# A transformer block for 16 batches on one core: the order of loads and weight preparation ahead of batch 0

## The reference, cut to what matters

```python
x = x + 0.5 * ffn(layernorm(x))
x = x + attention(layernorm(x))      # 16 heads of 16, rope on q and k, softmax, output projection
x = x + 0.5 * ffn(layernorm(x))
# ffn(x), for each batch:
base = x @ W_base + b_base
h = relu(x @ W_enc[n] + b_enc[n])                    # 8 autoencoders n
recon = h @ W_dec[n] + b_dec[n]
n = argmin over n of mean((recon - x) ** 2)          # the adapter for this batch
out = base + relu(x @ W_down[n] + b_down[n]) @ W_up[n] + b_up[n]
```

## Time and profile before

| what | value |
|---|---|
| median of 3 timed runs | 2045.04 us (2039.3 to 2045.09) |
| the profiled execution | 2036.09 us |
| its span, first to last instruction | 2034.3 us |
| PE busy | 1819.5 us, 89% |
| DVE busy | 1287.8 us, 63% |
| ACT busy | 986.9 us, 49% |
| POOL busy | 516.8 us, 25% |
| mean granted TensorE clock | 0.967 |
| DMA packets, bytes | 96685, 99.72 MB |

### The profile page before, as it was taken

How to read it: one execution, slowest core, us unless ns; L and a number is a source line. 1 busy time by engine, 2 the same in 40 slices (tenths; PEclk the granted TensorE clock), 3 DMA queues, 4 the chain that set the end, 5 groups by cost and what they waited for, 6 DMA issues and landing times.

```text
span 2034.3 us, 29855 instructions
## 1 busy us (share of the span) xinstructions
PE 1819.5 (89%) x9128; PEld 999.1 (49%) x9128; DVE 1287.8 (63%) x2796; ACT 986.9 (49%) x1953; POOL 516.8 (25%) x664
## 2 busy tenths in 40 slices
PE   2669898999989999899989999899998999998885
PEld 1543545555454545445455554545455454544344
DVE  6357665766757676666757667576766766665631
ACT  0125465555635555454545556355553645464541
POOL 3131314141221414122141412214141221413101
PEclk9879999999999999899999999999998999999897
DMA  4050505032150503205050321405041050504100
GB/s 105 11 94 11 94 11 96 9 66 50 29 88 12 104 4 74 41 19 97 12 105 1 66 50 31 86 12 104 12 72 35 23 93 12 104 1 89 16 11 11
DMA packets 96685, 99.72 MB, mean 49 GB/s; under 512 B 19970, under 2 KB 88195, under 8 KB 96387
## 3 DMA queue, kind: packets, MB, share of 16 engines
q1 hardware_dynamic: 96516, 97.66, 25.5%
HBM read 63.54 MB, written 33.55 MB: 48 GB/s over the span
## 4 chain that ended last, share of the span: by engine, by line
PE 62%; DVE 11%; DMA 9%; issue 8%; ACT 4%; SPq 4%; POOL 2%; POOLq 0%; DVEq 0%; ACTq 0%
PE ps L510 10%; PE ps L498 9%; PE ps L577 8%; PE ps L488 8%; PE ps L556 6%; DMA scratch<-parts 5%; DVE mx L816 5%; PE ps L565 4%; PE ps L613 4%; SPq L473 3%; DMA out_dram<-x 3%; PE ps L629 3%; PE ps L674 2%; ACT pr L709 2%; PE ps L616 2%
## 5 line engine op out<-in xcount | busy, mean ns | idle before, releaser
L816 DVE TENSOR_REDUCE mx<-ps 128x1 f32<-128x512 f32 x1024 | 655.0, 685 | 271.4 <-PE ps L488 268.8
L709 ACT ACTIVATE pr<-ps 128x512 f32<-128x512 f32 x1024 | 555.9, 598 | 284.8 <-PE ps L498 284.2
L488 PE MATMUL ps<-stack 96*128 96x512 bf16 x1024 | 326.8, 388 | 58.6 <-issue 34.0
L498 PE MATMUL ps<-stack 98*128 98x512 bf16 x1024 | 320.7, 384 | 19.5 <-ACT pr L709 10.4
L510 PE MATMUL ps<-pr,va 128*32 128x512 f32 x2048 | 272.5, 604 | 4.6 <-ACT pr L709 4.6
L762 ACT ACTIVATE h<-ps,benc 128x512 f32<-128x512 f32 x128 | 88.0, 687 | 271.6 <-PE ps L556 271.6
L498 PEld LDWEIGHTS ps<-stack 98*128 98x128 bf16 x1024 | 77.6, 100 | 269.3 <-ACT pr L709 173.0
L488 PEld LDWEIGHTS ps<-stack 96*128 96x128 bf16 x1024 | 96.8, 98 | 218.7 <-DVE mx L816 89.3
L868 DVE SCALAR_TENSOR_TENSOR ps<-ps,wb,h 128x512 f32<-128x512 f32 x128 | 96.7, 756 | 149.9 <-PE ps L565 149.9
L1009 POOL TENSOR_SCALAR rs<-mv 128x4 f32<-128x4 f32 x48 | 11.5, 241 | 651.0 <-DVE mv L836 651.0
L556 PE MATMUL ps<-xh,w_eh 128*128 128x512 f32 x256 | 121.1, 473 | 17.8 <-issue 11.3
(11 more groups left out here) (155 smaller groups left out, 2995.1 us busy)
## 6 DMA issues: line engine op xcount, KB each, us to landing
stack<-scratch SPq DMA_DIRECT2D x384, 128.0 KB, 4.4
scratch<-parts SPq DMA_DIRECT2D x64, 384.0 KB, 5.4
xin<-in_L_attn_x_dram SPq DMA_DIRECT2D x16, 512.0 KB, 3.5
out_dram<-x SPq DMA_DIRECT2D x16, 512.0 KB, 6.0
stack<-wu_mT SPq DMA_DIRECT2D x128, 4.0 KB, 1.7
cst<-in_const_dram SPq DMA_DIRECT2D x1, 1024.0 KB
raw<-in_L_ffn_W_dec_dram SPq DMA_DIRECT2D x1, 512.0 KB, 5.5
pr<-in_L_ffn_W_enc_dram SPq DMA_DIRECT2D x2, 256.0 KB, 5.5
```

Source lines behind the costliest of these rows:

```text
L488: pe.matmul(bank1[:, t % 2, :], stack[b.odd][0][0:KB, hd, 128 * t:128 * t + 128], stack[b.odd][1][0:KB, hd, :], start=True, stop=True).the ...
L498: pe.matmul(bank2[:, a % 2, :], stack[b.odd][1][:, 4 * g + a, 128 * t:128 * t + 128], stack[b.odd][0][:, 4 * g + a, :], start=True, stop=T ...
L709: act.activation(pr[:, n % 2, a, :], bank2[:, a % 2, :], ACT.Exp, scale=SCALE).then_inc(ex_done.sem, 1)
L816: dve.tensor_reduce(mx[:, hd // 4 % 2, e:e + 1], bank1[:, t % 2, :], AX.X, ALU.max).then_inc(mx_done.sem, 1)
```

## The change

- The loads of the first group get semaphores of their own. SP issues x, the tables (s_ident), both parts of W_enc and benc (s_enc), then the 18 loads of s_rest. ScalarE issues W_dec, both parts of bdec and cidx (s_decoder).
- The two rows of -1 in stack are no longer filled by GpSimd. GpSimd fills 2 x 256 elements, and two transfers at the end of SP's opening copy them out (s_rows). TensorE and ScalarE wait for these ahead of the first L498 and the first maxima.
- ScalarE makes w_eh, as soon as W_enc is there; VectorE makes w_el.
- The rest of VectorE's opening becomes two steps of the walk of pass -1: w1 (decoder weights, cidx, b_base) ahead of the first decoder product, and w2 (splits of W_base, Wq, Wk, Wv) behind the choice. The waits for s_split move to the first up product (2) and the first q product (3).
- GpSimd's remaining fills stand ahead of its work on rs.

```diff
@@ schedule
+            if at == (2, 0) and initial(n): step("w1")       # behind zs, ahead of gr
             if at == (6, 1):
                 step("cost", n, 0)
                 step("pick", n, 0)
+                if initial(n): step("w2")
@@ macaron
+        minus = mT[0:2].rearrange("p k q -> p (k q)")
@@ sync
-                bring(s_first, cst[:, 0:tables], const[:, 0:tables])
-                bring(s_first, benc[:], b_enc.rearrange("(p e) r -> (e r) p", e=2))
-                bring(s_first, cidx[:].bitcast(I32), connected_idx.partition_broadcast(128))
...
+                bring(s_ident, cst[:, 0:tables], const[:, 0:tables])
+                for c in range(C):
+                    bring(s_enc, w_e[:, c], W_enc[:, 128 * c:128 * c + 128, :].rearrange("n p r -> p n r"))
+                bring(s_enc, benc[:], b_enc.rearrange("(p e) r -> (e r) p", e=2))
...
+                sp.wait_ge(s_fill, 1)
+                for o in range(2):
+                    bring(s_rows, stack[o][1][KB:KB + 2, :, :].rearrange("p h (a x) -> p (h a) x", x=2 * 128),
+                          minus.unsqueeze(1).to_broadcast([2, 2 * H, 2 * 128]))
@@ tensor
+                if initial(b) and n == 0 and half == 0:      # s2
+                    pe.wait_ge(s_rows, 32)
...
-            pe.wait_ge(s_first, 16 * FIRST_LOADS)
+            pe.wait_ge(s_ident, 16)
+            pe.wait_ge(s_decoder, 16 * DECODER_LOADS)
@@ scalar
+            act.dma_start(w_dec, W_dec.rearrange("(a b) r d -> (b r) a d", b=2)).then_inc(s_decoder, 16)
+            with nc.allow_non_contiguous_dma(reason="small bias columns, once"):
+                for c in range(C):
+                    act.dma_start(bdec[:, c], b_dec[:, 128 * c:128 * c + 128].rearrange("n p -> p n")).then_inc(s_decoder, 16)
+                act.dma_start(cidx[:].bitcast(I32), connected_idx.partition_broadcast(128)).then_inc(s_decoder, 16)
+            act.wait_ge(s_enc, 16 * ENC_LOADS)
+            act.copy(w_eh[:], w_e).then_inc(s_high, 1)
             enter(do)
@@ vector
+            def decoder_weights():          # w1
+                # ident_b, w_dh, w_dl, bd_sum, gram_w filled with 0, wait s_wt 2, wb2 and gram_w (16 small
+                # copies), power, s_ready 1, cidx, wait s_rest, wu_all + b_base, s_ready 2
+            def dense_weights():            # w2
+                # w_bh, w_bl, s_split 2, then the pairs of Wq, Wk, Wv, s_split 3
             dve.memset(power[:], -0.5).then_inc(s_const, 1)
-            dve.wait_ge(s_first, 16 * FIRST_LOADS)
-            link(dve.tensor_copy(ident_b[:], ident))
             enter(do)
...
+            dve.wait_ge(s_decoder, 16 * DECODER_LOADS)
             link(dve.tensor_scalar(bdec[:], bdec[:], -2.0, None, ALU.mult))
             dve.wait_ge(s_wt, 1)
             link(dve.tensor_copy(raw[:, 2, :], ps[:, 0, :]))
             dve.tensor_copy(raw[:, 3, :], ps[:, 1, :]).then_inc(s_dec, 1)
...
+            dve.wait_ge(s_high, 1)
+            dve.tensor_tensor(w_el[:], w_e, w_eh[:].bitcast(F32), ALU.subtract).then_inc(s_split, 1)
             walk(dve, do)
@@ gpsimd
+            pool.memset(minus, -1.0).then_inc(s_fill, 1)
+            pool.wait_ge(s_fill, 1)
+            pool.memset(mid[R:R + 1, :], 1.0).then_inc(s_fill, 1)
+            pool.wait_ge(s_fill, 2)
+            pool.memset(va[:, :, :, HD:2 * HD], 1.0).then_inc(s_fill, 1)
             pool.wait_ge(s_const, 1)
             enter(do)
-
-            pool.wait_ge(*rs_done[0].at(Batch(0, 0), 0))
-            pool.memset(mid[R:R + 1, :], 1.0).then_inc(s_fill, 1)
...
-                pool.memset(stack[o][1][KB:KB + 2, :, :], -1.0).then_inc(s_fill, 1)
```

More of the change, by code:

```diff
@@ L401, in macaron @@
         passed = sem("passed")
-        s_first = sem("s_first")
+        s_ident = sem("s_ident")
+        s_enc = sem("s_enc")
+        s_decoder = sem("s_decoder")
         s_rest = sem("s_rest")
+        s_rows = sem("s_rows")
+        s_high = sem("s_high")
         s_const = sem("s_const")
@@ L411, in macaron @@
         s_ready = sem("s_ready")
-        FIRST_LOADS, REST_LOADS = 8, 18
+        ENC_LOADS, DECODER_LOADS, REST_LOADS = 3, 4, 18
+        w_dec = raw[:, 0:2, :].rearrange("p a (b c) -> p (a b) c", c=D)
+        w_decT = raw[:, 2:4, :]
         block = ctx.enter_context(nc.Block())
@@ L622, in project @@
                 if k == 0:
+                    if initial(b):
+                        pe.wait_ge(s_split, 3)
                     pe.wait_ge(*xl_done[2].at(b, C - 1))
@@ L721, in maxima @@
                 bank = late
+                if initial(b) and g == 0:
+                    act.wait_ge(s_rows, 32)
                 act.wait_ge(*mt_full.at(b, g))
@@ L950, in out_project @@
                    .then_inc(x2_done.sem, 1)
+            def decoder_weights():
+                link(dve.tensor_copy(ident_b[:], ident))
+                link(dve.tensor_scalar(w_dh[:], w_decT, -2.0, None, ALU.mult))
+                link(dve.scalar_tensor_tensor(out=w_dl[:], in0=w_decT, scalar=-2.0, in1=w_dh[:].bitcast(F32), op0=ALU.mult,
+                                              op1=ALU.subtract))
+                sq = key[0]
+                link(dve.tensor_tensor(sq[:], bdec[:], bdec[:], ALU.mult))
+                link(dve.tensor_tensor(bd_sum[:], sq[:, 0, :], sq[:, 1, :], ALU.add))
+                link(dve.tensor_scalar(bd_sum[:], bd_sum[:], S / 4.0, None, ALU.mult))
+                link(dve.memset(gram_w[:], 0.0))
+                dve.wait_ge(s_wt, 2)
+                for p in range(NP):
+                    for e in range(2):
+                        q = slice(R * e, R * e + R)
+                        dve.tensor_scalar(wb2[q, p:p + 1], ps[q, 3, 10 * p + e:10 * p + e + 1], -1.0, None, ALU.mult)
+                        dve.tensor_copy(gram_w[q, p, R * e:R * e + R], ps[q, 2, 128 * p + R * e:128 * p + R * e + R])
+                link(dve.tensor_copy(power[:], power[:]))
+                dve.tensor_copy(power[:], power[:]).then_inc(s_ready, 1)
+                link(dve.tensor_copy(z[0][:], cidx[:].bitcast(I32)))
+                link(dve.tensor_scalar(z[1][:], z[0][:], 0.0, float(N), ALU.is_lt, ALU.mult))
+                link(dve.tensor_tensor(z[0][:], z[0][:], z[1][:], ALU.add))
+                link(dve.tensor_scalar(cidx[:], z[0][:], 0.0, float(N - 1), ALU.max, ALU.min))
+                dve.wait_ge(s_rest, 16 * REST_LOADS)
+                dve.tensor_tensor(wu_all[R:R + 1], wu_all[R:R + 1],
+                                  x2[R:R + 1, 0:1, :].to_broadcast([1, N, D]), ALU.add).then_inc(s_ready, 1)
@@ new lines, in dense_weights @@
+            def dense_weights():
+                link(dve.tensor_copy(w_bh[:], w_b))
+                dve.tensor_tensor(w_bl[:], w_b, w_bh[:].bitcast(F32), ALU.subtract).then_inc(s_split, 1)
+                for raw_w, w in ((q_raw, w_q), (k_raw, w_k), (v_raw, w_v)):
+                    link(dve.tensor_copy(w[0][:], raw_w))
+                    last = dve.tensor_tensor(w[1][:], raw_w, w[0][:].bitcast(F32), ALU.subtract)
+                    if w is not w_v:
+                        link(last)
+                last.then_inc(s_split, 1)
@@ L962, in _ @@
-            dve.tensor_tensor(w_el[:], w_e, w_eh[:].bitcast(F32), ALU.subtract).then_inc(s_split, 1)
+            dve.wait_ge(s_decoder, 16 * DECODER_LOADS)
             link(dve.tensor_scalar(bdec[:], bdec[:], -2.0, None, ALU.mult))
[L965 to L968, removed]
             dve.wait_ge(s_wt, 1)
```

21 lines of the change are left out of this document (5 added, 16 removed).

## The result

| | before | after |
|---|---|---|
| median of the timed runs | 2042.17 us (4: 2036.6 to 2045.09) | 2004.75 us (4: 2002.29 to 2008.66) |
| ratio of the times | | 0.9818, 95% interval 0.9801 to 0.9836 |
| the profiled execution, its span | 2036.09, 2034.3 us | 2006.59, 2004.8 us |
| first encoder matmul of batch 0 | 54.12 us | 18.51 us |
| first down matmul (L599, now L608) | 77.99 us | 40.87 us |

The kernel is 37.4 us faster; 33.9 were forecast, and a time of 2010.

The account below looks back on a forecast made before the run. The prediction took the opening's chain of waits up to batch 0's first encoder matmul as what the change could shorten: 34.0 - 0.6 + 0.5 = 33.9 us saved, 2045.0 less that 2011.1, said as 2010, range 2000 to 2022.

Parts of the forecast that it names:

- The sum: Whole kernel: 34.0 us from the opening, less 0.6, plus 0.5, makes 33.9 us saved; time given as 2010.
- Part 1, the fill: Four xn normalisations in the opening: without GpSimd's fills beside them 1.6 us instead of 15.76, so 14.2 us go.
- Rival C: Opening's xn stall is not the fill's but DMA traffic's: 21 us saved, time 2024; chance 0.03.
- Part 2, the loads: Opening's loads: x at 4.6, decoder group at 9.0, first encoder matmul at 20.1 instead of 54.12, 34.0 us saved.
- rival A: Opening's loads come no earlier, since two queues share the engines: 29.5 to 31 us saved, 2014 to 2016; chance 0.13.
- The cover of xl and w_el: Ahead of the first encoder matmul: xl ready at about 16.6 and w_el at 13.3, both 3 us early.
- Parts 2 and 5, TensorE's rate: Gram products 7.0 us as now; first encoder matmuls start less slowly without the pause, gain 0 to 2.0, taken 0.5.
- Part 3, w1: Decoder weights inside VectorE's walk: hidden, 5.9 us of cover on TensorE, 4 us ahead of VectorE's first decoder product.
- rival B: Hidden work comes out, by late rest loads or the choice beside the splits: 3 to 6 us less saved; chance 0.08.
- Part 4, w2: Dense weight splits behind the choice: hidden, but slow GpSimd's choice instructions by 0 to 2.3 us, taken 0.6.
- Rival D, the seams: Seams between batches run longer at 1.2 GHz: slower, 6 us more each at half rate gives 2056; chance 0.04.

Follow-up runs that it names:

- second traces: The kernel before and the kernel after, each run again unchanged: 2042.38 us (ratio 1.0001) and 2005.35 us (ratio 0.9826).
- one queue: Kernel after, but SyncE issues all loads, W_dec, bdec and cidx behind the tables and ahead of W_enc: 1999.97 us, run again 2004.99 us.
- fills alone: Kernel before, with GpSimd's two fills of 2 x 8192 replaced by two transfers and its other fills ahead of rs: 2030.22 us, ratio 0.9945.
- pause: Kernel after, with one VectorE copy ahead of the Gram products made four times, for 2.1 us more: 2005.81 us.
- halves: Kernel after, x split over both queues, first transposes awaiting W_dec and tables, benc on ScalarE's queue, Wq, Wk, Wv splits behind the choice: 2007.42 us, ratio 0.9839.
- weight work ahead: Kernel after, with both weight steps (w1 and w2) called ahead of VectorE's walk, ahead of xl: 2022.16 us, run again 2019.58 us.

## Why the prediction was right, point by point

**The sum.** 33.9 us forecast, 37.4 measured (interval 33.5 to 40.6 by the ratio), and the sign, the place and the mechanism were as said. The first down matmul came 37.1 us earlier, and in the second traces 78.52 - 41.29 = 37.2. The 37.1 are 35.6 to the first encoder matmul (54.12 - 18.51; 34.0 forecast), 2.1 in the encoder (0.5 forecast) and 0.6 given back at the choice. The 35.6 are two errors of opposite sign on the forecast start of 20.1: the transposes began 2.0 us late and took 0.5 less, and the Gram products took 3.1 less. So part of the nearness is luck. The medians with the traces' openings taken off show no loss behind the opening (an estimate, since only the profiled executions have a known opening): 2042.5 - 1.8 - 78.3 = 1962.4 us of body before, 2005.35 - 1.8 - 41.1 = 1962.5 after. The 2010 was 5.3 too high: 3.5 from the gain, 2.9 from a median of before that came out as 2042.2 instead of 2045.0, less the 1.1 by which 2010 was set under the sum.

**Part 1, the fill.** Right: xn 1.39 us, and both ways of testing it gave 13.6 to 14.3 us in the trace for 14.2. Rival C (the stall is the load traffic's) is out. The Trainium skill's page SBUF — State Buffer, section "SBUF: two separate sides", has VectorE and GpSimd share one pair of ports there, one holding it while the other waits; of VectorE's instructions with one input it says this for those that run in a two-port mode. These traces agree on the wait, with 15.76 us beside the fills and 1.38 without; the mode of an instruction stands in none of them.

**Part 2, the loads.** The term that was mis-sized in one direction: x was taken at 4.6 and came at about 6.0, the decoder group at 9.0 and came at 10.9. On this landing rival A (12.0) was nearer than the forecast (9.0), though not on the time. x took 5.3 us to land where it had taken 3.5. The 4.6 rested on ScalarE needing 1.46 us to issue W_dec; it needed 0.51, and x came at the forecast's own upper bound, 6.1, at which W_dec's 512 KB travel beside it. The bytes fit: the DMA engines moved 1130 KB up to the landing of x, which is about x, W_dec and the tables, and 700 KB with one queue, where x took 3.7 us (view by stretch, the kernel after, then one queue):

```profile
1.50:6.04 4.54, 0.00 (x0) 0.00 (x0) 0.00 (x0) 0.00 (x0) 1.07 (x2) 1.00 0.83 249
```

```profile
1.50:4.40 2.90, 0.00 (x0) 0.00 (x0) 0.00 (x0) 0.52 (x1) 1.08 (x2) 1.00 0.77 241
```

What the small loads add to that isn't separated. With all loads on one queue x was earlier, and so were the first transposes, which wait for the decoder group (9.39 and 10.10 against 11.05 and 11.19). So the second queue brought nothing to these two (W_enc it brought 0.9 us sooner); what the opening won from the loads is left to their order and to what each engine waits for. The cover of xl and w_el, taken as 3 us, was 1.0 (xl done at 17.49, the Gram products at 18.5).

**Parts 2 and 5, TensorE's rate.** The term that was mis-sized in the other direction, and it outweighed the first. The Gram products were taken at 7.0 us "as now", with 0.5 us for the encoder. They took 3.9, and the encoder 5.86 instead of 7.96 (the chain shows 5.71, since it gives the first 0.15 us to the Gram products). That is 2.1 us, a little more than the 2.0 that the forecast allowed at most, and 5.2 us together for the 0.5. The earlier trace rows had shown that TensorE worked slowly at first after a pause, and "the Gram products themselves never sped up" was read as a property of theirs, without asking what the 2.0 us pause ahead of them did. Over all traces: with a pause of 2 us or more directly ahead, the Gram products took 7.0 us in 5 of 5 (before twice, fills alone, pause, halves); with transposes running into them they took 3.7 to 4.5 in 7 of 9 and about 7.0 in 2 of 9, and both of these kernels had quick ones in their other trace. So a pause is enough for slow Gram products as far as five traces can show it, and it is not the only thing that gives them. The moment of the rise to the 2.4 GHz level (0.69 for four matmuls against 1.20) differs from execution to execution of one kernel. What decides it isn't shown.

**Part 3, w1.** Right in kind, thin in size. The forecast had 5.9 us of cover ahead of the first decoder matmul and 4 ahead of VectorE's first decoder product. With the faster TensorE, and VectorE's part done at about the forecast time, the first shrank to 25.2 - 23.8 = 1.4 us and the second to 27.85 - 27.39 = 0.5. In the one-queue kernel the second was gone, which is rival B: of the 1.8 us by which its first encoder matmul was earlier, 1.1 were lost by the first down matmul.

**Part 4, w2.** Right: 0.6 us taken, 3.06 - 2.46 = 0.60 measured, and moving the splits gave it back. That it fits to the tenth is luck, since the bounds were 0 and 2.3.

**Rival D, the seams.** It did not turn the sign, but the body varies more than was thought. The bodies of all traces lie between 1955.7 and 1967.6 us, and those of one kernel 0.0 to 4.7 apart. This is why the two spans of the table differ by 29.5 us and the medians by 37.4: the first trace of before has a body of 1956.3, the first of after 1963.9. In the second pair of traces the spans differ by 34.3; both profiled executions of before were under the median of their kernel (2036.09 and 2041.27), both of after above it (2006.59 and 2006.98). An example of low clock is one stretch near the end of the kernel after:

```profile
1840.00:1880.00 40.00, 29.05 (x91) 12.50 (x91) 22.43 (x43) 11.80 (x27) 5.65 (x11) 0.66 0.38 63
```

The mean granted clock was 0.966 and 0.967 in the traces with bodies of 1955.9, 1956.3 and 1958.5 us and 0.962 to 0.964 in those with 1963.9, 1964.4 and 1967.6, but also 0.961 in one with 1959.4 (weight work ahead, second trace) and 0.965 in the shortest, 1955.7 (one queue, first trace). So long bodies mostly go with a lower clock, but what fixes either for an execution stays open, and so does why the kernel with the pause lost 6.9 us in its opening and only 1.1 in its time.

**Where the 37.1 us came from**, by the traces: 14 from the fills and 16 from the weight work inside the walk (part of it TensorE's slow start, which comes back with the pause), each measured by putting it back into the kernel after. The remaining 7 or so fall to the loads' order, the earlier wait for x and the faster Gram products; this is a remainder, since no run puts the old load order back, and the three are not told apart.

## What to carry to other kernels

In an opening, order the work by what the next engine waits for and look for the wait, not for the busy share: of the 37 us here 14 were VectorE held by a neighbour's fill, and some 16 VectorE work that nobody wanted yet. When a gap in front of TensorE closes, cost the work behind the gap anew, since a duration measured after a pause may be of the lower clock. Covers shrink with it: take the slack from the faster schedule, not from the old one.

## What the runs showed of the hardware that was not expected

- GpSimd's fill of two partitions x 8192 elements took 6.96 us, and that of 128 partitions x 1024 elements 0.98 us: here (bf16 in the one, f32 in the other) the time went by the elements along the partition and not by their sum. The long one held a VectorE instruction of 0.40 us for its whole length (7.1 us).
- The holding goes the other way too. In the eight traces in which VectorE's b_base add of 2.28 us (L998) overlapped GpSimd's offsets, one of these took 2.2 to 2.35 us beside it: L1088 in the first trace of the kernel after, L1083, otherwise 0.20 us, in the second (timeline, second trace, below). In both traces of the one-queue kernel the offsets were done before the add began, and none stood.

```profile
24.80 2.35 POOL L1083 TENSOR_TENSOR zt<-zt 128x8 f32<-128x8 f32 x1
24.80 2.28 DVE L998 TENSOR_TENSOR wu_all<-wu_all,x 1x2048 f32<-1x2048 f32 x1 [0.19 <-DMA b_bc<-in_L_attn_b_dram]
```

- The issue of a small load can itself stand: cidx took ScalarE 3.99 us to issue and benc SyncE 3.64, against 0.50 and 0.43 in the kernel before.
- One kernel, executed twice, ran the same Gram products in 7.0 us once and in 4.3 once, though their starts lay 0.1 us apart (14.84 and 14.74).
